# A two-layer attention kernel: ten second-layer groups normalised by transfers, products issued in pairs

## The reference

```
ss = cond @ w_cond;  scale, shift = ss[:, :c], ss[:, c:]
xm = rms(x) * rms_w * (1 + scale) + shift
q, k, v = split(xm @ w_qkv);  q, k = rope(q), rope(k)
o = softmax(q k / 4) v
x = o @ w_out + residual
```

```
xn = layer_norm(x);  q, k, v = xn @ q_w + q_b, xn @ k_w + k_b, (xn @ v_w + v_b) * mask
y = softmax(q k + (1 - mask) * -1e6) v
e = silu(emb) @ emb_w + emb_b;  scale, shift = split(e)
h = layer_norm(y) * (1 + scale) + shift
x = x + silu(h) @ out_w + out_b
```

## Time and profile before

| | us |
|---|---|
| median of 3 runs (lowest, highest) | 493.04 (492.73, 493.89) |
| the profiled execution | 493.28 |
| its span | 491.5 |
| TensorE busy | 479.5 (98%) |
| VectorE busy | 386.1 (79%) |
| ScalarE busy | 342.7 (70%) |
| Pool busy | 314.2 (64%) |
| chain that ended last, share of TensorE | 79% |
| the same, VectorE | 14% |

### The profile page before, as it was taken

How to read it: one execution, slowest core, us unless ns; L and a number is a source line. 1 busy time by engine, 2 the same in 40 slices (tenths; PEclk the granted TensorE clock), 3 DMA queues, 4 the chain that set the end, 5 groups by cost and what they waited for, 6 DMA issues and landing times.

```text
span 491.5 us, 9721 instructions
## 1 busy us (share of the span) xinstructions
PE 479.5 (98%) x3205; PEld 178.4 (36%) x3205; DVE 386.1 (79%) x990; ACT 342.7 (70%) x676; POOL 314.2 (64%) x447
## 2 busy tenths in 40 slices
PE   7999899999999999999999999999999999999996
PEld 3563322323333334333343234333333323333234
DVE  3767896998886688856887688967899999999224
ACT  1662467898767786867767776776787778777853
POOL 6569976888798898699737692739991055005501
PEclk9999999999999999999999999999999999999999
DMA  7775157444423365225412361104411121111011
GB/s 244 197 206 194 45 135 264 112 115 149 112 66 115 111 183 149 68 68 140 123 54 67 107 187 44 46 24 126 114 45 44 45 88 45 44 45 45 2 43 43
DMA packets 41577, 49.79 MB, mean 101 GB/s; under 512 B 12388, under 2 KB 34036, under 8 KB 41272
## 3 DMA queue, kind: packets, MB, share of 16 engines
q1 hardware_dynamic: 33336, 31.84, 22.6%
q0 software_dynamic: 7904, 16.03, 10.9%
q10 hardware_dynamic: 288, 1.31, 0.8%
HBM read 27.62 MB, written 19.01 MB: 95 GB/s over the span
## 4 chain that ended last, share of the span: by engine, by line
PE 79%; DVE 14%; issue 3%; POOL 2%; ACT 1%; DVEq 0%; POOLq 0%; ACTq 0%
PE bank L602 20%; PE bank L648 12%; PE bank L576 11%; PE bank L585 11%; PE bank L564 9%; DVE masked L958 8%; PE bank L659 6%; PE bank L676 5%; DVE row_max L961 2%; PE bank L633 2%; ACT probs L787 1%; PE bank L617 1%; PE bank L610 1%; PE bank L734 1%; POOL shift L1335 1%
## 5 line engine op out<-in xcount | busy, mean ns | idle before, releaser
L787 ACT ACTIVATE probs<-bank 128x512 f32<-128x512 f32 x512 | 270.2, 599 | 71.3 <-PE bank L576 70.6
L961 DVE TENSOR_REDUCE row_max<-bank 128x1 f32<-128x512 f32 x256 | 159.9, 681 | 38.1 <-PE bank L585 37.9
L585 PE MATMUL bank<-k_s,q_s 64*128 64x512 f16 x512 | 179.9, 382 | 2.1 <-DVE row_max L961 1.2
L958 DVE CUSTOM_DVE_ANT_0 masked<-bank,mask_bias 128x512 bf16<-128x512 f32 x256 | 162.1, 687 | 20.3 <-PE bank L585 19.6
L564 PE MATMUL bank<-q_s,k_s 64*128 64x512 f16 x512 | 151.3, 380 | 0.3
L576 PE MATMUL bank<-shift,kx 64*128 64x512 f16 x512 | 148.7, 376 | 0.0
L602 PE MATMUL bank<-probs,v_aug 128*17 128x512 f32 x1024 | 135.4, 598 | 0.7 <-ACT probs L787 0.7
L585 PEld LDWEIGHTS bank<-k_s,q_s 64*128 64x128 f16 x512 | 46.2, 93 | 154.6 <-DVE row_max L961 67.4
L1238 POOL TENSOR_SCALAR scaled<-row_max 128x16 f32<-128x16 f32 x30 | 7.7, 256 | 86.3 <-DVE row_max L958 49.0
L648 PE MATMUL bank<-xT,wqkv 128*128 128x512 f32 x128 | 59.6, 605 | 1.0 <-DVE xT L1095 0.6
L576 PEld LDWEIGHTS bank<-shift,kx 64*128 64x128 f16 x512 | 46.9, 95 | 33.4
(11 more groups left out here) (122 smaller groups left out, 480.6 us busy)
## 6 DMA issues: line engine op xcount, KB each, us to landing
q_s<-q_parts SPq DMA_DIRECT2D x32, 256.0 KB, 3.3
k_s<-k_parts SPq DMA_DIRECT2D x32, 256.0 KB, 4.4
k_parts<-parts POOLq DMA_DIRECT2D x62, 128.0 KB, 3.2
q_parts<-parts POOLq DMA_DIRECT2D x60, 128.0 KB, 3.0
X<-in_x SPq DMA_DIRECT2D x4, 512.0 KB, 7.1
O<-oT SPq DMA_DIRECT2D x64, 32.0 KB, 2.0
roped<-inverses SPq DMA_DIRECT2D x16, 128.0 KB
y<-X SPq DMA_DIRECT2D x7, 256.0 KB, 2.2
```

The lines of the kernel that those rows point to most:

```text
L585: nc.tensor.matmul(bank, m.q_s[slot][rows, i, queries], m.k_s[slot][rows, i, :], start=True, stop=True).then_inc(q.d_made, 1)
L787: act.activation(m.probs[k][:, h, :], bank, ACT.Exp, scale=1.0 if s >= B * NG else float(DH) ** -0.5)\
L958: dve.tensor_tensor_reduce(m.masked[D["max", n, k, h] % ND][:, :], bank, m.mask_bias[:, b, :], 1.0, LOWEST, ALU.add, ALU.max, to)\
L961: dve.tensor_reduce(to, bank, AX.X, ALU.max).then_inc(q.d_done, 1)
```

## The change

`SENT` = 26 is new: groups up to 25 go by transfers, ten of layer 1 among them (16 to 25). In these groups ScalarE, not SyncE, issues the transfer of the sums, for layer 0 too: 26 times, behind its copy. In layer 0 VectorE still inverts. In layer 1 Pool does, by a power of -1 on 128 x 16 (`invert`), and multiplies the raw output in place (`divide`). TensorE turns each chunk back into rows of tokens (piece `back`, four transposes) and ScalarE copies it to `tokens`, which lies where `wc` was. A batch has two chunks: there are `back` pieces for batches 0 and 1, and one for batch 2, of whose groups 26 and 27 go by transposes as before. The halves of v and of the y of layer 0 are put into one tile each. The statistics of a batch come together. The conditioning is turned by transposes and summed by VectorE; in the opening ScalarE makes one of the four normalised tiles.

```diff
-    _other = v(0, 3)[1:] if _b == 0 else v(1, _b - 1)[1:]
-    PIECES[_s] = (*one(y(0, _b)), _other, ())
+    PIECES[_s] = ((), y(0, _b), v(1, _b - 1) if _b else v(0, 3), ())
     PIECES[_s + 1] = ((), (), turn("p1", _b), qk(1, _b, 0, 1))
     PIECES[_s + 2] = ((), qk(1, _b, 2, 3), (), ())
-    PIECES[_s + 3] = (v(1, _b)[:1], (), (), ())
-PIECES[20] = ((), qk(1, LAST, 2, 3), (), v(1, LAST)[:1])
-PIECES[21] = (v(1, LAST)[1:], (), (), ())
...
-PIECES[23] = ((), (), y(1, 0)[:1], ())
-PIECES[24] = ((), (), (), y(1, 0)[1:])
-PIECES[26] = (*one(turn("f1", 1)), (), ())
-PIECES[27] = ((), (), y(1, 1)[:1], ())
-PIECES[28] = ((), (), (), y(1, 1)[1:])
+
+PIECES[20] = ((), qk(1, LAST, 2, 3) + (("back", 0, 0),), (), ())
+PIECES[21] = ((), (), (("back", 0, 1),), v(1, LAST))
+PIECES[23] = (*one(turn("f1", 0)), (), (("back", 1, 0),))
+PIECES[24] = ((), (), y(1, 0)[:1], ())
+PIECES[25] = ((), (), (("back", 1, 1),), y(1, 0)[1:])
+PIECES[27] = (*one(turn("f1", 1)), (), (("back", 2, 0),))
+PIECES[28] = ((), (), y(1, 1)[:1], y(1, 1)[1:])
...
-    STATISTICS[6 + NG * _b, 1] = ("p1", _b, 0)
-    STATISTICS[6 + NG * _b, 2] = ("p1", _b, 1)
-for _b in range(B - 1):
-    STATISTICS[20 + NG * _b, 3] = ("f1", _b, None)
+    STATISTICS[6 + NG * _b, 2] = ("p1", _b)
+for _b, _s in enumerate((21, 25, 28)):
+    STATISTICS[_s, 3] = ("f1", _b)
...
+SENT = LAYER + NG * (B - 2) + NG // 2
...
-        if op == "output" and k == 2 and s > LAYER:
+        if op == "output" and k == 2 and s > SENT:
...
+    def turn_back(piece):
+        _, b, c = piece
+        bank = a_free(A[piece])
+        pe.wait_ge(q.divided, normalised(B + b, c))
+        for t in range(TPB):
+            last = nc.tensor.transpose(bank[:, t * P:(t + 1) * P], m.raw[b % 2][:, c, t * P:(t + 1) * P], m.ident[:, :])
+        last.then_inc(q.a_made, 1)
...
-            pe.wait_ge(q.chosen_step, B)
+            pe.wait_ge(q.ident_made, 4)
             pe.wait_ge(q.a_done, A[kind, 0] + 1)
             for c in range(KC):
-                last = nc.tensor.matmul(bank[:, c * B:(c + 1) * B], m.conditions[:, c * P:(c + 1) * P], m.chosen[:, :],
-                                        start=True, stop=True)
+                last = nc.tensor.transpose(bank[:, c * P:(c + 1) * P], m.conditions[:, c * P:(c + 1) * P], m.ident[:, :])
...
-        if s > LAYER:
+        if s > SENT:
             act.wait_ge(q.d_made, D["output", s - 1] + 1)
         elif s:
             act.wait_ge(q.output_out, group_out(s - 1))
             act.wait_ge(q.sums_in, 16 * s)
         act.activation(m.oT[:, :], m.ACC, ACT.Copy).then_inc(q.acc_copied, 1)
+        if s < SENT:
+
+            act.wait_ge(q.acc_copied, s + 1)
+            if s:
+                act.wait_ge(q.inv_made, s)
+            act.dma_start(m.sums[:, :], m.oT[DH::W32, :].rearrange("h (c n) -> h c n", n=KT * G)).then_inc(q.sums_in, 16)
...
+    def back(piece):
+        _, b, c = piece
+        bank = made(A[piece])
+        if b >= 2:
+            act.wait_ge(q.xn_made, TPB * NORMAL.index(("f1", b - 2)))
+        act.activation(m.tokens[b % 2][:, :, c * P:(c + 1) * P], bank.rearrange("p (t n) -> p t n", n=P), ACT.Copy)\
+            .then_inc(q.a_done, 1)
...
+        if op == "sums" and at[0] < LAYER:
             invert(*at)
...
+    def divide(pu, c):
+
+        layer, b = divmod(pu, B)
+        pool.wait_ge(q.output_out, group_out(NG * pu + 2 * c + 1))
+        pool.wait_ge(q.inv_in[c], 32 * (pu + 1))
+        to = raw = m.raw[b % 2][:, c, :]
+        if layer == 0:
+            use = USES.index(("f0", b))
+            await_read(pool, q, use - 2)
+            to = m.xT[use % 2][:, c, :]
+        pool.tensor_tensor(to, raw, m.inverse[c][:, :], ALU.mult).then_inc(q.divided, 1)
+
+    def invert(s):
+
+        pool.wait_ge(q.sums_in, 16 * (s + 1))
+        pool.wait_ge(q.inv_out, 16 * s)
+        pool.tensor_tensor(m.inv_sum[:, :, :, :].rearrange("p t h w -> p (t h w)"), m.sums[:, :], m.minus_one[:, :],
+                           ALU.pow).then_inc(q.inv_made, 1)
...
+        dve.tensor_reduce(m.mod0[:, :, :], by_chunk(made(D["modulate", 1])), AX.X, ALU.add).then_inc(q.mod_made, 1)
...
@@ -1381,16 +1428,24 @@
         .then_inc(q.mask_step, 1)
     rope(2, 0, 3)
     rope(2, 1, 4)
-    rope(2, 2, 5)
+    rope(2, 2)
+    negate(5)
     rope(2, 3)
     negate(6)
     divide(0, 0)
+    rotate(3, 0)
     divide(0, 1)
-    rope(3, 0, 7)
-    rope(3, 1, send=False)
+    rotated_parts(3, 0, 7)
+    rope(3, 1)
 
...
@@ -1430,48 +1484,77 @@
     split(B, 2)
     negate(11)
     split(B, 3)
-    add_bias(0, 0)
     for b in range(1, LAST):
         normalise(b)
         divide(b + 1, 0)
         if b == 1:
             add_output_bias(0)
         add_output_bias(b)
-        add_bias(b - 1, 1)
+        add_bias(b - 1, 0)
...
         split(B + b, 3)
-        add_bias(b, 0)
         divide(b + 1, 1)
+        add_bias(b - 1, 1)
...
+
+    pool.wait_ge(q.one_made, 1)
+    invert(16)
+    invert(17)
+    normalise(LAST)
+    divide(B, 0)
...
+    negate(21)
+    split(B + LAST, 0)
+    split(B + LAST, 1)
+    invert(19)
+    negate(22)
+    divide(B, 1)
+    invert(20)
+    split(B + LAST, 2)
+    split(B + LAST, 3)
+    negate(23)
...
-    def sums(s):
...
-        sp.dma_start(m.sums[:, :], m.oT[DH::W32, :].rearrange("h (c n) -> h c n", n=KT * G)).then_inc(q.sums_in, 16)
...
-        if b >= 2:
+        if b >= B + 2:
+            sp.wait_ge(q.a_made, A["back", b - 2 - B, g // 2] + 1)
+        elif b >= 2:
             sp.wait_ge(q.divided, normalised(b - 2, g // 2))
```

More of the change, by code:

```diff
@@ L196, in key_tile @@
                 yield "piece", piece
-        if op == "output" and k == 2 and s > LAYER:
+        if op == "output" and k == 2 and s > SENT:
             yield op, s - 1
-        if op == "output" and k == 3 and 0 < s <= LAYER:
+        if op == "output" and k == 3 and 0 < s <= SENT:
             yield "sums", s - 1
@@ L374, in build @@
         m.wc = sb("wc", [P, KC, COND])
+        m.tokens = [m.wc[:, 2 * i:2 * i + 2, :].rearrange("p k n -> p (k n)").rearrange("p (t c) -> p t c", c=C)
+                    for i in range(2)]
         m.vb_row = sb("vb_row", [P, C])
@@ L759, in tensor @@
                 turn_tokens(piece)
+            if piece[0] == "back":
+                turn_back(piece)
             if piece[0] == "qk":
@@ L916, in scalar @@
                 tokens(piece)
+            if piece[0] == "back":
+                back(piece)
             if piece[0] == "qk":
@@ L922, in scalar @@
                 conditions(piece)
+            if piece == ("modulate", 0):
+                act.wait_ge(q.rstd0_made, 1)
+                act.activation(m.XN[0][:, TPB - 1, :], m.X[:, TPB - 1, :], ACT.Copy,
+                               scale=m.rstd["p0"][:, TPB - 1:TPB]).then_inc(q.xn0_made, 1)
             if piece == ("qk", 0, 1, 3):
@@ L992, in write_output, with statistics @@
         dve.wait_ge(q.inv_made, s + 1)
-        dve.tensor_tensor(m.O[pu % 2][:, :, g * G * DH:(g + 1) * G * DH].rearrange("p t (h d) -> p t h d", d=DH),
+        dve.tensor_tensor(m.tokens[pu % 2][:, :, g * G * DH:(g + 1) * G * DH].rearrange("p t (h d) -> p t h d", d=DH),
                           bank[:, :, :, 0:DH], m.inv_sum[:, :, :, :].broadcast_to([P, KT, G, DH]), ALU.mult)\
            .then_inc(q.d_done, 1)
-    def statistics(kind, b, src, t0, tiles):
-        for t in range(t0, t0 + tiles):
+    def statistics(kind, b, src):
+        for t in range(TPB):
             stat(dve.bn_stats(m.stats[:, TPB * b + t, :], src(t)))
@@ L1032, in opening @@
         dve.wait_ge(q.rstd0_made, 1)
-        for t in range(TPB):
+        for t in range(TPB - 1):
             normal_tile(dve, m, "p0", m.X[:, 0:TPB, :], m.XN[0], t, t).then_inc(q.xn0_made, 1)
@@ L1175, in vector @@
                 negate(n)
-        if op == "sums":
+        if op == "sums" and at[0] < LAYER:
             invert(*at)
@@ L1262, in split, with rotate @@
         send_parts(pu, i)
-    def rope(b, i, *shifts, send=True):
+    def rotate(b, i):
         side, two = divmod(i, 2)
@@ L1284, in rope @@
             negate(n)
-        if send:
-            send_parts(b, i)
+        send_parts(b, i)
+    def rope(b, i, *shifts):
+        rotate(b, i)
+        rotated_parts(b, i, *shifts)
     def add_bias(b, j):
@@ L1450, in gpsimd, with silu @@
             modulation()
-    normalise(LAST)
-    add_output_bias(LAST)
-    add_bias(LAST - 1, 1)
-    negate(NG * LAST + 9)
-    for i in range(4):
-        split(B + LAST, i)
-    for b in range(LAST):
-        negate(NG * (B + b) + 6)
-        rstd("f1", b)
-        normal("f1", b)
-        if b == 0:
-            add_bias(LAST, 0)
-        negate(NG * (B + b) + 7)
-        if b == 0:
-            add_bias(LAST, 1)
+    def silu(b):
         for h in range(CT):
@@ L1471, in gpsimd @@
             pool.tensor_tensor(m.xT[i][:, h, :], m.tanh[h], m.halved[h], ALU.mult).then_inc(q.silu_made, 1)
-        for n in (NG * (B + b) + 8, NG * (B + b) + 9):
-            if n in POOL_SHIFTS:
```

(36 more changed lines are left out.)

106 lines of the change are left out of this document (47 added, 59 removed).

## The result

The changed kernel takes 504.88 us (median of 4 runs, 504.26 to 505.08) against 492.88 (492.56 to 493.89, 4 runs of the same chip). The ratio is 1.0239, 95% interval 1.0225 to 1.0253: slower by 12.0 us. Forecast were 501.1 and a range of 488.5 to 505. The median lies 0.1 us inside the upper end of that range, and one of the four runs (505.08) outside it. The profiled execution has a span of 503.1 us, 11.6 more than before.

The account below looks back on a forecast made before the run. TensorE, busy 98% of the span, was taken as the bound. From 493.28 us, gains of 5.6 and losses of 10.4 (issue) and 3.3 (Pool) gave 501.4, as a median 501.1 us, range 488.5 to 505.

Parts of the forecast that it names:

- Gains on TensorE: TensorE: fewer output turns 5.83, pairs 2.34, conditioning turn 0.4, less 3.01 for chunks turned back: 5.6 us gained.
- rival C: Issue delays ScalarE only about 0.1 us, L610 has slack, Pool comes in time, gains stand: 489.1 us; chance 0.16.
- Loss 1: Tile 1: issuing the sums holds ScalarE 0.50 us before the exponentials; 17 tiles lose 0.61 each, 10.4 us.
- counted as covered: Nine of 26 tiles 1, step 23 among them, hold a piece before L610 that hides the issue: no loss there.
- The table load of the earlier trace: ScalarE's opening: it starts 0.03 us after a 0.40 us transfer issue ends, taken to show that issuing holds ScalarE.
- Loss 2: Step 24, tile 1: ScalarE waits for Pool's power of group 22 before issuing the next sums, 3.3 us.
- the line through two narrow ones: Pool's power on 128x16, extrapolated from 128x4 at 1044 ns and 128x2 at 712 ns: 3.0 us.
- the two ways through DRAM: Layer 1: inverses travel from Pool's power to the division, taken as 5.3 us, ends 4.6 and 6.0.
- Rival D: Issue is free but Pool's power takes 3 us, TensorE waits 4.5 in step 24: 493.6 us; chance 0.12.
- B: Rival: the issue holds ScalarE, but Pool's power is quick (1.04 us): 497.8 us; chance 0.14.
- A: The forecast itself: ScalarE held by the issue and waiting for Pool, 501.1 us, ends 498 to 504.5; chance 0.50.
- E: Rival: Pool's lateness passes to its shifts of steps 23 to 26, with under 1 us of room: over 505; chance 0.08.

Follow-up runs that it names:

- both undone: Changed kernel with SyncE issuing the sums and VectorE inverting all groups; the fewer output turns, turns back and pairs stay: 491.73 us (0.9965).
- with the issue free and VectorE inverting: Changed kernel with VectorE inverting all groups and ScalarE issuing the sums behind the first two exponentials of tile 1: 491.37 us (0.9965).
- the experiment on the kernel before: The kernel before with only its 16 transfers of the sums issued by ScalarE behind its copy instead of by SyncE: 499.52 us (1.0131).

## Why the prediction was right

**Gains on TensorE, 5.6 us: right for this kernel.** 6.5 by the difference. The opening, named and not counted, gave 0.5, and a wait of 0.45 for Pool in step 7 has gone, which wasn't foreseen; the pairs gave 0.20 instead of 0.26 each, 0.5 less. The half microsecond that is left isn't assigned. The gains stand whole only beside the losses: with both undone TensorE loses 4.2 us to waits for Pool and VectorE that the forecast put at nothing, and is 1.2 us ahead of the kernel before. The forecast of rival C, 489.1, took them as whole; with the issue free and VectorE inverting the kernel takes 491.4.

**Loss 1, 10.4 us: right in place, 2.0 short in size.** The issue took 0.53 to 0.56 us (0.50 taken, between 0.40 and 0.61) and a tile lost 0.65 (0.61): 17 x 0.65 = 11.1. The first issue took 0.6 longer, and step 23, counted as covered, lost 0.7. Together 12.4; the experiment on the kernel before shows this loss by itself. The reason given was only half of it: "ScalarE is held while it issues" is true behind a wait for its own last instruction and false two instructions later. The table load of the earlier trace rows, on which I rested it, had nothing queued in front of it either. Rival C wanted an issue below about 0.2 us; none took less than 0.53. Its premise that an issue costs ScalarE nearly nothing holds two exponentials later and not in this place.

**Loss 2, 3.3 us: right in kind, near in size partly by luck.** The power took 2.93 us where the line through two narrow ones gave 3.0; ScalarE waited 3.7. But the two ways through DRAM took 6.0 and 6.5 us (346.33 to 352.37 and 375.09 to 381.55), not 5.3, and by the prediction's own ends 6.0 made the wait 4.7. That it stayed at 3.7 is due to TensorE, which was late too: counted from the start of group 19's last value products (334.42) the copy ended at 54.3 instead of 52.9, and the power at 58.0 instead of 56.2. Rival D fell with the row of the issue and B with the row of the power.

**What the forecast lacked, 2.0 us:** the slower clock behind the long gap, 1.6, and the wait of the turned chunk, 0.4 (priced only as a part of loss 2). 2.0 + 0.4 + 2.0 - 0.9 gained more = 3.5, nearly the 3.8 us between 501.1 and 504.9. The misses in the losses all went the same way, 4.4 us together, more than the 3.9 between forecast and upper end; only the larger gains brought the time back. That it lies 0.1 us inside the range is luck, and it is above the ends given for A (498 to 504.5). E's place, the shifts of steps 23 to 26, was not reached here; it was in the kernel where SyncE issues.

**What it had not seen at all** is that the two losses cover each other. Taken singly it would have priced the removal of the issue at 10.4 us; it is worth 3.6 (504.9 to 501.3) while Pool inverts, and 8.9 when it doesn't.
